# Norm rows and the stacks of attention B turned by transfers instead of by TensorE

## The chip, the cores and the metric
The kernel runs on one core of one Trainium2 chip. The metric is device time in microseconds (us), the time of one execution on that core. Five engines work side by side, each with its own instruction stream: TensorE (PE; its weight loads are listed as PEld), VectorE (DVE), ScalarE (ACT), GpSimd (POOL) and SyncE (SP), which here only issues transfers. They wait for each other through semaphores. All engines read and write the on-chip memory SBUF; PE writes its results to the eight banks of PSUM (`bank[0]` to `bank[7]`, 128 partitions x 512 float32 each).

## The reference, cut to what matters
The input x has 2 sequences of 512 tokens with 512 columns. Four layers are added to it in turn, each on the normalized rows of x:

```python
x = x + attention_a(_layernorm(x), ...)   # 32 heads of 128, 8 KV heads, weights as 4-bit codes with scales
x = x + ffn(_layernorm(x), ...)           # 8 experts of rank 64, the 2 best per token
x = x + attention_b(_layernorm(x), ...)   # 32 heads of 16, 8 KV heads
x = x + ffn(_layernorm(x), ...)           # the same experts once more
```

Attention B is `q, k, v = xn @ Wq, xn @ Wk, xn @ Wv`, a rotation of q and k (`q * cos + rotate_half(q) * sin`), causal softmax attention and `@ Wo`. The expert layer is `gate_probs = softmax(xn @ gate_w.T)`, the two largest of 8, and the weighted sum of `xn @ lora_A[e].T @ lora_B[e].T`.

## The kernel before, in words
**Tiles and precision.** The 1024 tokens are NT = 8 tiles of 128 rows (t = 0 to 7; ST = 4 per sequence). A matrix product takes the tokens as columns, so each normalized tile has to be turned from [128 tokens, 512] to four blocks [128 columns, 128 tokens]. Products run as three float16 products: each value is split into a high half (a float16 copy) and a low half (the value less the copy), and `three` issues high x high, high x low, low x high. `xt` holds the turned rows, halves `xt_hi` and `xt_lo`.

**Norm rows, for layer c = 0 to 3.** `ln_stats` (DVE) takes mean and variance, `ln_rsqrt` (POOL) the factor, `ln_norm` (DVE, L1549) writes the normalized tile to `xn` in SBUF. Then `ln_t` (PE, L1036) turns it by four transposes into a PSUM bank, `ln_hi` (ACT, L740) copies the bank to `xt_hi` and `ln_lo` (DVE, L1554) makes `xt_lo`.

**Order of work.** Each engine's order is written out by hand. First comes attention A, in groups j = 0 to 7, one per KV head; its probabilities are already turned by transfers on SP's queue (`turn_head`, L476: 20 blocks of 128 x 128 float16 each, from `p_row` to `p_turned`; the profile names these tiles `bw_hi` and `bw_lo`, with which they share memory). Its last products (`a_out`) are added to x by `o_add` (DVE) for t = 3 to 7.

Then `experts(0)`: for each t PE does `ln_t` of the next tile, the gate product (12 matmuls of 8 columns) and the product with `lora_a` (12 matmuls of 512 columns); ACT copies it to `hidden`. DVE chooses the experts for half of the tiles at a time (`gate_choice`, `gate_weights`), and POOL's `weighted` multiplies `hidden` by the weights into `hs` (L650). In a second loop PE turns `hs` back (`turn`, L1231) and multiplies by `lora_b` (`second`); DVE adds the result to x (`y_add`) and takes the next layer's statistics. On POOL, `largest` (L622) reduces the largest weight of a lot over the partitions, for the factors by which DVE's `w_factors` scales the weights; `w_scale` and `w_high` (ACT) and `w_low` (POOL, L630) then make the halves of the weights.

Then the projections of attention B. For each t PE computes `b_q` (12 matmuls of 512 columns) and `b_kv` (12 of 256). DVE's `rope_products` (L1922, L1923) makes the rotation's products in `rq1`, `rq2`, `rk1`, `rk2` (two buffers each, t % 2). POOL adds them (L678, L680). ACT's `stack_high` copies the high half twice to `q_stack` (L978) and four times to `k_stack` (L982), and POOL writes the low half twice to `q_stack` (L684) and four times to `k_stack` (L689). `stack_t` (PE, L1308) turns the 24 blocks in six units of four, through PSUM banks, and `stack_out` on ACT (L994) and DVE (L1931) copies them to `qt_b` and `kt_b`. Between the steps stand `ln_t`, `ln_hi` and `ln_lo` of tile t + 2 and the first score steps (`b_scores` on PE, `b_max` on DVE).

Then attention B itself runs in 16 sets q (sequence q // 8): `b_scores` and `b_max` find the row maxima, `b_split` (POOL) and `b_turn_max` turn them, `b_keys` and `b_exps` (ACT) make the probabilities in `pt`, and `b_pv` multiplies by v. The first `b_keys` with a maximum is the PE instruction of L1358 for set 0. The first sets need only the tiles 0 to 3. Last come the product with `b_o` and `experts(1)`, on rows of layer c = 3.

Of the kernel before, what the change touches and what calls it, by code (L numbers as in the profile page):

```python
# [24 lines left out]
P = 128  # L25
# [69 lines left out]
LN_BANK = [(0, 1, 0, 1, 6, 7, 6, 6), (2, 3) * 4, (3, 4) * 4, (3, 4) * 4]  # L95

HALF = NT // 2
GATE_BANK = [5, 7]
# [87 lines left out]


UNITS = 6
ACT_UNITS = (0, 1, 4, 5)


def t_bank(t, unit):

    return ((2, 7) if t < NT - 2 else (5, 7))[unit % 2]


def act_units(t, unit):

    before = len(ACT_UNITS) * min(t, NT - 2) + UNITS * max(t - (NT - 2), 0)
    return before + (unit + 1 if t >= NT - 2 else ACT_UNITS.index(unit) + 1)  # L200


def dve_units(t, unit):

    return 2 * t + unit - 1


def build(nc, t_in, out):
    ctx = ExitStack()
    with ctx:  # L210
# [85 lines left out]
        scn = sa("scn", [P, sum(QUANT_COLS.values())], F32)  # L296
# [8 lines left out]
        arena = sa("arena", [P, 10 * 1024], F32)  # L305
        q_hi = arena[:, 0:2048].bitcast(F16).rearrange("p (s n) -> p s n", s=8)
# [50 lines left out]
        rk1 = staged("rk1", [P, 2, P], F32)  # L357
        rk2 = staged("rk2", [P, 2, P], F32)
# [5 lines left out]
        ctx_t = sb("ctx_t", [P, S], F32)  # L364
# [42 lines left out]
        d_turned = [sem(f"d_turned{i}") for i in range(2)]  # L407
# [10 lines left out]
        bkept, zeros_done, bt_ps, bt_act, bt_dve = (sem(n) for n in ("bkept", "zeros_done", "bt_ps", "bt_act", "bt_dve"))  # L418
# [15 lines left out]
        def load_scales(eng, n, j):  # L434
# [13 lines left out]
        def _(sp):  # L448
# [41 lines left out]
        def _(pool):  # L490
# [142 lines left out]
            for t in range(ST):  # L633
                ln_rsqrt(1, t)
            w_low("lora_a", 0, 1)
            w_low("gate", 0, 1)

# [19 lines left out]
            for t in range(ST, NT):  # L657
                ln_rsqrt(1, t)
            w_low("lora_b", 0, 1)

            largest(1)
            pool.wait_ge(wlo_done, 3)
# [5 lines left out]
            pool.memset(bv[:, :, KV_HEADS * B_VD:], 0.0).then_inc(zeros_done, 1)  # L668
            weighted(0)
            w_low("b_o", 0, 1)  # L670
            for t in range(NT):
                ln_rsqrt(2, t)


            for t in range(NT):
# [39 lines left out]
            def b_keep(q, kt, loads):  # L715
# [3 lines left out]
                home = GROUP * (q % 2)  # L719
# [17 lines left out]
        def _(act):  # L737
            def ln_hi(c, t):
                act.wait_ge(xt_ps, NT * c + t + 1)
                act.activation(xt_hi[:, :, t * P:(t + 1) * P],  # L740
                               bank[LN_BANK[c][t]][:].rearrange("p (k n) -> p k n", k=KT),
                               ACT.Copy, scale=X_UP).then_inc(xthi_done, 1)

# [20 lines left out]
            for t in range(ST):  # L764
                ln_hi(0, t)
# [25 lines left out]
            def b_exps(q, which):  # L791


                home = GROUP * (q % 2)
# [54 lines left out]
            def group(j, first, last):  # L849
# [15 lines left out]
                if first:  # L865
                    ln_hi(0, ST + 3)
# [1253 lines left out]
```

## Time and profile before

| | us |
|---|---|
| median of 3 runs | 1022.82 (1020.14 to 1024.01) |
| the profiled execution, its own time | 1022.0 |
| its span, first to last instruction | 1020.3 |
| PE busy | 953.5 (93%) |
| DVE, POOL, ACT busy | 795.7, 629.8, 612.7 |

The times of all rows below are in us from the start of the span. Stretches, as the traced instructions mark them: attention A up to 693.6, experts(0) up to 751.7, projections of attention B up to 808.1 (the first `b_keys` with its maximum), attention B and its output up to 966.9, experts(1) up to the end. Busy time of an engine is not what sets the end: the chain of work that ended last, and the waits in it, do.

### The profile page before, as it was taken

Reading aid. Unit: us, or ns where it says so; the run is one execution under the profiler, and the core shown is the slowest. Engines: PE = TensorE matmul, PEld = TensorE weight load, DVE = VectorE, ACT = ScalarE, POOL = GpSimd, SP = SyncE. Lnnn points to the kernel's source line nnn. Section 1 sums busy time; section 2 is a strip of 40 time slices with the busy share of each in tenths; the row PEclk is TensorE's granted clock in tenths of the full one; section 3 lists DMA queues with packets and bytes.
Section 4 is the critical chain, followed back from the end, with each engine's and each line's share of the span. In section 5 each row is a group of like instructions: output and inputs, shape, how many; then the busy total and the mean of one; then the engine's idle time right before and its main releaser. Section 6 shows DMA issues by size and latency. Waiting matters only on the chain.

```text
span 1020.3 us, 20687 instructions
## 1 busy us (share of the span) xinstructions
PE 953.5 (93%) x7235; PEld 520.7 (51%) x7235; DVE 795.7 (78%) x1860; ACT 612.7 (60%) x1346; POOL 629.8 (62%) x643
## 2 busy tenths in 40 slices
PE   3698999999999999999999999868999799999998
PEld 1244555555555555555555555534456444444554
DVE  6877887887887887887888788758687789995744
ACT  2267666676666766667667665552637688886131
POOL 3767876967868768777777776213578444443111
PEclk9989999999999999999999999979999999999999
DMA  8164474364474473663653564520000000000002
GB/s 287 49 186 131 98 193 129 84 197 120 83 201 106 107 202 78 134 185 69 161 164 90 140 151 83 156 52 1 1 1 2 2 2 2 3 2 1 1 1 83
DMA packets 179892, 95.22 MB, mean 93 GB/s; under 512 B 168032, under 2 KB 168544, under 8 KB 175200
## 3 DMA queue, kind: packets, MB, share of 16 engines
q1 hardware_dynamic: 170016, 49.44, 22.3%
q10 hardware_dynamic: 9792, 44.59, 13.5%
q8 instruction: 62, 1.02, 0.4%
q14 instruction: 22, 0.18, 0.1%
HBM read 49.97 MB, written 2.10 MB: 51 GB/s over the span
## 4 chain that ended last, share of the span: by engine, by line
PE 76%; DVE 9%; POOL 5%; issue 5%; ACT 4%; DMA 1%; SPq 0%; ACTq 0%; DVEq 0%; POOLq 0%
PE bank L1026 15%; PE bank L1028 15%; PE bank L1027 15%; PE bank L1445 4%; PE bank L1113 3%; PE bank L1115 3%; PE bank L1114 3%; PE bank L1133 3%; PE bank L1135 3%; PE bank L1134 3%; PE bank L1353 2%; PE bank L1334 2%; PE bank L1358 2%; DVE bank L1656 1%; ACT bank L788 1%
## 5 line engine op out<-in xcount | busy, mean ns | idle before, releaser
L537 POOL TENSOR_TENSOR rt<-rt 128x512 f32<-128x512 f32 x80 | 101.1, 1268 | 137.8 <-DVE rt L1641 137.8
L1673 DVE SCALAR_TENSOR_TENSOR bw_hi<-bank,rden,bw_hi 128x128 f16<-128x128 f32 (+3 forms) x256 | 123.3, 544 | 61.3 <-ACT bw_hi L819 61.3
L788 ACT ACTIVATE bank<-bank,shift,c_score 128x128 f32<-128x128 f32 (+3 forms) x256 | 147.3, 605 | 2.1
L1656 DVE CUSTOM_DVE_ANT_0 bank<-bank,mask_w 128x512 f32<-128x512 f32 (+3 forms) x256 | 117.9, 518 | 21.7 <-PE bank L1115 21.4
L819 ACT ACTIVATE bw_hi<-bank,rden 128x128 f16<-128x128 f32 (+3 forms) x256 | 114.5, 536 | 25.3 <-DVE rden L1666 25.2
L783 ACT ACTIVATE shift<-smax,c_score 128x4 f32<-128x4 f32 x64 | 19.0, 297 | 163.3 <-DVE smax L1656 163.3
L1026 PE MATMUL bank<-xt,wq_hi 128*128 128x512 f16 x256 | 98.8, 386 | 2.2 <-DVE rt L1641 1.8
L1027 PE MATMUL bank<-xt,wq_hi 128*128 128x512 f16 x256 | 98.6, 385 | 0.0
L1028 PE MATMUL bank<-xt,wq_lo 128*128 128x512 f16 x256 | 98.5, 385 | 0.0
L1026 PE MATMUL bank<-wo_hi,arena 128*128 128x512 f16 x256 | 97.5, 381 | 0.6 <-DVE x L1685 0.6
L1027 PE MATMUL bank<-wo_lo,arena 128*128 128x512 f16 x256 | 97.5, 381 | 0.0
L1028 PE MATMUL bank<-wo_hi,arena 128*128 128x512 f16 x256 | 97.3, 380 | 0.0
L544 POOL TENSOR_TENSOR arena<-rt,arena 128x512 f16<-128x512 f32 x80 | 92.3, 1158 | 6.4 <-ACT arena L772 5.7
L800 ACT ACTIVATE pt<-bank,c_score_b 128x512 f32<-128x512 f32 x128 | 81.1, 686 | 19.9 <-PE bank L1358 19.5
L1113 PE MATMUL bank<-arena 128*128 128x512 f16 (+3 forms) x256 | 74.7, 304 | 16.5 <-DVE bw_hi L1673 8.7
L1133 PE MATMUL bank<-bw_lo,arena 128*128 128x512 f16 (+3 forms) x256 | 77.2, 302 | 7.5 <-DMA bw_lo<-bw_hi 7.1
L1114 PE MATMUL bank<-arena 128*128 128x512 f16 (+3 forms) x256 | 77.8, 304 | 0.0
L1134 PE MATMUL bank<-bw_lo,arena 128*128 128x512 f16 (+3 forms) x256 | 77.3, 302 | 0.0
L1115 PE MATMUL bank<-arena 128*128 128x512 f16 (+3 forms) x256 | 75.0, 304 | 0.0
L1135 PE MATMUL bank<-bw_lo,arena 128*128 128x512 f16 (+3 forms) x256 | 74.0, 302 | 0.0
L1639 DVE TENSOR_TENSOR rt<-bank,sin_a 64x512 f32<-64x512 f32 x80 | 55.4, 693 | 20.6 <-PE bank L1028 18.7
L1958 DVE TENSOR_REDUCE smax_b<-bank 128x2 f32<-128x1024 f32 (+1 forms) x64 | 58.6, 951 | 13.8 <-PE bank L1319 13.8
(235 smaller groups left out, 2597.1 us busy)
## 6 DMA issues: line engine op xcount, KB each, us to landing
qcode<-in_q_codes ACTq DMA_DIRECT2D x8, 1024.0 KB, 5.0
qscale<-in_q_scales ACTq DMA_DIRECT2D x8, 1024.0 KB, 7.8
ocode<-in_o_codes ACTq DMA_DIRECT2D x7, 1024.0 KB, 4.9
oscale<-in_o_scales ACTq DMA_DIRECT2D x7, 1024.0 KB, 8.7
kvcode<-in_k_codes ACTq DMA_DIRECT2D x8, 256.0 KB, 8.7
kvcode<-in_v_codes ACTq DMA_DIRECT2D x8, 256.0 KB, 9.0
kvscale<-in_k_scales ACTq DMA_DIRECT2D x8, 256.0 KB, 8.9
kvscale<-in_v_scales ACTq DMA_DIRECT2D x8, 256.0 KB, 9.2
```

Source lines behind the costliest of these rows:

```text
L788: act.activation(a_rows(i, s), a_rows(i, s), ACT.Exp, bias=shift[:, s % 2, c:c + 1], scale=c_score[:, 0:1], accum_out=bank[3][:, SUMS_AT + ...
L819: act.activation(p_row[:, s % 2, HI_AT[i]:HI_AT[i] + P_STEP * i + 1:P_STEP], turned_back(i, s), ACT.Copy, scale=rden[:, s % 2, c:c + 1]).t ...
L1026: pe.matmul(out_ap, a_hi, b_hi, start=(k == 0), stop=False)
L1027: pe.matmul(out_ap, a_hi, b_lo, start=False, stop=False)
L1028: return pe.matmul(out_ap, a_lo, b_hi, start=False, stop=(stop and k == n - 1))
L1113: pe.matmul(o_ap, q_hi[:, s, qs], k_hi[:, b, 0:w], start=True, stop=False)
L1114: pe.matmul(o_ap, q_hi[:, s, qs], k_lo[:, b, 0:w], start=False, stop=False)
L1115: mm = pe.matmul(o_ap, q_lo[:, s, qs], k_hi[:, b, 0:w], start=False, stop=True)
L1133: pe.matmul(o_ap, v_hi[:, b, vs], hi, start=(kt == 0), stop=False)
L1134: pe.matmul(o_ap, v_hi[:, b, vs], lo, start=False, stop=False)
L1656: dve.tensor_tensor_reduce(bank[bk][:, o:o + (i + 1) * P], bank[bk][:, o:o + (i + 1) * P], mask_w[:, S - (i + 1) * P:S], 1.0, LOWEST, ALU. ...
L1673: dve.scalar_tensor_tensor(out=p_row[:, s % 2, LO_AT[i]:LO_AT[i] + P_STEP * i + 1:P_STEP], in0=turned_back(i, s), scalar=rden[:, s % 2, c: ...
```

## The change
- `ln_norm` for c = 1 to 3 writes to a PSUM bank (`XN_BANK`), not to `xn`. `row_hi` (ACT) and `row_lo` (DVE) write both halves, still row by row, to the new SBUF tile `rows` (two buffers), and `turn_rows` turns a tile's 8 blocks by one transfer on SP's queue straight into `xt`. PE waits for the landing (`d_rows`). `ln_t`, `ln_hi` and `ln_lo` stay for c = 0 alone.
- In the projections `turn_stacks` turns `q_stack` (16 blocks) and `k_stack` (8 blocks) by two transfers into `qt_b` and `kt_b`. `stack_t`, both `stack_out` and `ident_h` are gone. A buffer of a stack is written again only when its transfer has landed (`d_q`, `d_k`).
- POOL makes the low half of the queries once (512 elements, not 1024), and ACT's new `stack_again` copies it to the second place.
- Orders change with it. `w_factors(0)` moves behind `probs_low(7)`; the reductions of the second lot of weights (`w_largest`) spread out; the second `largest` moves behind the memsets; `w_low` of `lora_a`, `lora_b` and `b_o` goes in quarters between the `ln_rsqrt`. The gate and weights of `experts` come in another order on DVE: `m_low` of the second tile goes ahead of the second `gate_weights`. The first three score steps' `b_max` run after all rotations, not between them.
- Memory: `rk1`, `rk2` and `ctx_t` move into `hs`, `scn` into `arena`, and the sets' places in `pt` are swapped so that set 0 doesn't touch the stacks.

```diff
+XN_BANK = {1: (3, 2), 2: (3, 4), 3: (4, 3)}
-GATE_BANK = [5, 7]
+GATE_BANK = [(7, 4), (5, 7)]
+        rows = sb("rows", [P, 2, 2, D], F16)
-        ident_h = sb("ident_h", [P, P], F16)
+        def rows_landed(c, t):
+            return 16 * (HALF * (c - 1) + t // 2 + 1)
...
+            def turn_rows(c, t):
+                sp.wait_ge(xt_done, NT * c + t + 1)
+                sp.dma_start_transpose(xt[:, :, :, t * P:(t + 1) * P].rearrange("p i k n -> p (i k) n"),
+                                       rows[:, t % 2].rearrange("p i n -> p (i n)")).then_inc(d_rows[t % 2], 16)
+            for t in range(NT):
+                turn_rows(1, t)
+            def turn_stacks(t):
+                ts = slice(t * P, (t + 1) * P)
+                sp.wait_ge(bq_lo, t + 1)
+                sp.dma_start_transpose(qt_b[:, :, ts], q_stack[:, t % 2]).then_inc(d_q[t % 2], 16)
+                sp.wait_ge(bk_lo, t + 1)
+                sp.dma_start_transpose(kt_b[:, :, ts], k_stack[:, t % 2]).then_inc(d_k[t % 2], 16)
+            for t in range(4):
+                turn_rows(2, t)
+            for t in range(NT):
+                if t + 4 < NT:
+                    turn_rows(2, t + 4)
+                turn_stacks(t)
+            for t in range(NT):
+                turn_rows(3, t)
...
-            largest(1)
-            pool.wait_ge(wlo_done, 3)
+            pool.wait_ge(wlo_done, 9)
             pool.memset(m_stack[:].rearrange("p i n -> p (i n)").bitcast(F32), 0.0).then_inc(zeros_done, 1)
...
+            largest(1)
             weighted(0)
...
-                rq = rq1[:, i2].rearrange("p (h d) -> p h d", d=B_HD).unsqueeze(2)
-                pool.tensor_tensor(st[:, :, 1], rq.broadcast_to([P, B_HEADS, 2, B_HD]), st[:, :, 0],
-                                   ALU.subtract).then_inc(bq_lo, 1)
+                pool.tensor_tensor(st[:, :, 1, 0], rq1[:, i2].rearrange("p (h d) -> p h d", d=B_HD), st[:, :, 0, 0],
+                                   ALU.subtract).then_inc(bq_once, 1)
...
+            def row_hi(c, t):
+                act.wait_ge(xn_ready, NT * c + t + 1)
+                if c > 1 or t >= 2:
+                    act.wait_ge(d_rows[t % 2], rows_landed(c, t) - 16)
+                act.activation(rows[:, t % 2, 0], bank[XN_BANK[c][t % 2]][:], ACT.Copy, scale=X_UP).then_inc(xthi_done, 1)
...
+            def stack_again(t):
+                act.wait_ge(bq_once, t + 1)
+                st = q_stack[:, t % 2].rearrange("p (h a e d) -> p h a e d", h=B_HEADS, a=2, e=2)
+                act.activation(st[:, :, 1, 1], st[:, :, 1, 0], ACT.Copy).then_inc(bq_lo, 1)
+            row_hi(2, 0)
+            row_hi(2, 1)
+            row_hi(2, 2)
             for t in range(NT):
...
+                if t + 3 < NT:
+                    row_hi(2, t + 3)
                 stack_high(t)
+                stack_again(t)
...
-            for t in range(ST, NT):
-                m_high(NT + t, 1.0)
+            row_hi(3, 0)
+            m_high(NT + ST, 1.0)
+            row_hi(3, 1)
+            m_high(NT + ST + 1, 1.0)
+            m_high(NT + ST + 2, 1.0)
+            row_hi(3, 2)
+            m_high(NT + ST + 3, 1.0)
+            row_hi(3, 3)
+            row_hi(3, 4)
             experts(1)
...
                 for t in range(NT):
-                    if t + 1 < NT and (ph == 0 or t):
-                        ln_t(c, t + 1)
-                    pe.wait_ge(xt_done, NT * c + t + 1)
+                    pe.wait_ge(d_rows[t % 2], rows_landed(c, t))
...
             for t in range(NT):
-                pe.wait_ge(xt_done, NT * 2 + t + 1)
+                pe.wait_ge(d_rows[t % 2], rows_landed(2, t))
...
-                wide(bank[t % 2][:], t, "b_q", D, range(0, 1))
-                if t >= 2:
-                    stack_t(t - 2, (2, 3))
...
+                wide(bank[t % 2][:], t, "b_q", D).then_inc(bq_ps, 1)
+                if t == NT - 1:
...
                     b_scores(0, 0, 3)
...
+            def row_lo(c, t):
                 dve.wait_ge(xthi_done, NT * c + t + 1)
+                dve.scalar_tensor_tensor(out=rows[:, t % 2, 1], in0=bank[XN_BANK[c][t % 2]][:], scalar=X_UP,
+                                         in1=rows[:, t % 2, 0], op0=ALU.mult, op1=ALU.subtract).then_inc(xt_done, 1)
...
                 row_factors(j, 7)
                 probs_low(j, 7)
                 ctx_low(j, "c", 5)
+                if last:
+                    w_factors(0)
...
+            row_lo(2, 2)
+            ln_norm(2, 3)
             for t in range(NT):
...
                 dve.wait_ge(bq_ps, t + 1)
                 if t >= 2:
                     dve.wait_ge(bk_lo, t - 1)
                 rope_products(bank[t % 2][:], rq1[:, t % 2], rq2[:, t % 2], t).then_inc(bq_mul, 1)
                 dve.wait_ge(bkv_ps, t + 1)
                 rope_products(bank[5 + t % 2][:, 0:P], rk1[:, t % 2], rk2[:, t % 2], t).then_inc(bk_mul, 1)
+                if t + 3 < NT:
+                    row_lo(2, t + 3)
+                if t + 4 < NT:
+                    ln_norm(2, t + 4)
+            b_max(0, 0, 3)
+            b_max(0, 0, 2)
+            b_max(0, 0, 1)
```

## Rows read from the trace of the kernel before

**Rows 1.** The page's part 4: shares of the chain that ended last.

```profile
PE 76%; DVE 9%; POOL 5%; issue 5%; ACT 4%; DMA 1%; SPq 0%; ACTq 0%; DVEq 0%; POOLq 0%
```

**Rows 2.** Windows view, two stretches: busy us (instructions) per engine, clock, DMA.

```profile
693.60:751.90 58.30, 52.85 (x362) 29.40 (x361) 46.15 (x113) 24.45 (x34) 29.68 (x30) 1.00 0.00 1
751.90:808.10 56.20, 52.23 (x482) 34.82 (x480) 41.17 (x88) 36.40 (x66) 42.09 (x38) 0.97 0.01 1
```

**Rows 3.** Timeline of PE, 669 to 723: start, us, instruction, [idle before <- releaser].

```profile
676.45 0.58 PE L1133 MATMUL bank<-bw_lo,arena 128*128 128x512 f16 x1 [7.08 <-DMA bw_lo<-bw_hi]
...
693.59 1.04 PE L1036 MATMUL bank<-ident,xn 128*128 128x128 f32 x8
...
696.33 0.18 PE L1026 MATMUL bank<-gate_hi,xt 128*128 128x8 f16 x1 [1.71 <-DVE xt L1554]
...
696.65 0.38 PE L1026 MATMUL bank<-lora_a_hi,xt 128*128 128x512 f16 x1
...
722.94 0.66 PE L1231 MATMUL bank<-ident,hs 128*128 128x128 f32 x4 [0.74 <-POOL hs L650]
```

**Rows 4.** Timeline of POOL around both partition reductions, same columns.

```profile
660.46 0.38 POOL L622 PARTITION_ALL_REDUCE pow_w<-amax_w  x1 [6.20 <-issue]
668.38 1.12 POOL L501 TENSOR_TENSOR rstd<-mv,minus_half 128x1 f32<-128x1 f32 x2 [7.54 <-DVE mv L1542]
...
712.19 0.39 POOL L622 PARTITION_ALL_REDUCE pow_w<-amax_w  x1 [11.85 <-DVE amax_w L1695]
...
720.38 1.24 POOL L665 TENSOR_TENSOR sel<-sel_f,one 128x640 bf16<-128x640 f32 x1 [7.54 <-issue]
```

**Rows 5.** Timeline of DVE ahead of row_factors(7) of the last group.

```profile
667.75 0.16 DVE L1526 TENSOR_SCALAR pow_w<-pow_w 128x3 f32<-128x3 f32 x1
...
668.94 0.15 DVE L1663 TENSOR_SCALAR rsum<-bank 128x4 f32<-128x4 f32 x1
```

**Rows 6.** The chain that ended last, in order of time: start, us, what.

```profile
733.26 0.44 PE bank L1231 x4
...
736.29 0.44 PE bank L1231 x4
...
756.05 1.28 POOL rq L678
```

**Rows 7.** Groups by form, POOL, 755 to 808 (busy us, mean ns, idle).

```profile
L684 POOL TENSOR_TENSOR q_stack<-rq,q_stack 128x1024 f16<-128x1024 f32 x8 | 17.1, 2134 | 5.9 <-ACT q_stack L978 5.9
L678 POOL TENSOR_TENSOR rq<-rq 128x512 f32<-128x512 f32 x8 | 10.3, 1290 | 2.6 <-DVE rq L1923 2.6
L689 POOL TENSOR_TENSOR k_stack<-rk,k_stack 128x512 f16<-128x512 f32 x8 | 9.3, 1158 | 0.0
```

**Rows 8.** Groups by form, ACT, the same stretch.

```profile
L978 ACT ACTIVATE q_stack<-rq 128x1024 f16<-128x1024 f32 x8 | 8.5, 1057 | 3.6 <-POOL rq L678 3.4
L982 ACT ACTIVATE k_stack<-rk 128x512 f16<-128x512 f32 x8 | 4.9, 618 | 0.0
```

**Rows 9.** Groups by form, DVE, the same stretch.

```profile
L1554 DVE SCALAR_TENSOR_TENSOR xt<-bank,xt 128x512 f16<-128x512 f32 x6 | 4.1, 681 | 0.0
```

**Rows 10.** All 64 transposing transfers: ns on SP's queue, and issue to landing.

```profile
L476 SPq DMA_TRANSPOSE bw_lo<-bw_hi x64: 2324/2587/10902, 52.3 to 672.2; - x64
...
DMA to landing us min/median/max: 4.1/4.3/13.1
```

**Rows 11.** Windows view, inside the landing of one such transfer.

```profile
674.00:675.00 1.00, 0.00 (x0) 0.00 (x0) 0.93 (x4) 0.00 (x0) 0.39 (x1) 0.50 1.27 290
```

**Rows 12.** Windows view, early in attention B.

```profile
814.00:820.00 6.00, 4.10 (x78) 2.43 (x74) 5.07 (x8) 5.06 (x8) 3.59 (x9) 1.00 0.00 0
```

**Rows 13.** Timeline of POOL: the last tile's low keys.

```profile
802.08 1.16 POOL L689 TENSOR_TENSOR k_stack<-rk,k_stack 128x512 f16<-128x512 f32 x1
```

**Rows 14.** Timeline of PE: set 0's first b_keys with its maximum.

```profile
808.09 0.39 PE L1358 MATMUL bank<-m_turned,sel 64*128 64x512 bf16 x2 [0.67 <-DVE m_turned L1965]
```

**Rows 15.** Timeline of DVE: the last m_low of the output product.

```profile
963.32 0.68 DVE L1861 SCALAR_TENSOR_TENSOR mt_lo<-bank,mt_hi 128x512 f16<-128x512 f32 x1
```

More of the change, by code:

```diff
@@ L930, in w_high @@
                 act.activation(w_hi[n][:], raw[n], ACT.Copy).then_inc(whi_done, 1)
-            for n in LOTS[0]:
-                w_scale(n)
-                w_high(n)
+            w_scale("lora_a")
+            w_high("lora_a")
+            row_hi(1, 0)
+            row_hi(1, 1)
+            ctx_high(KV_HEADS - 1, "cc", 7)
+            row_hi(1, 2)
+            w_scale("gate")
+            w_high("gate")
+            w_scale("lora_b")
+            row_hi(1, 3)
+            w_high("lora_b")
+            row_hi(1, ST)
             beside = [(w, n) for n in LOTS[1] for w in (w_scale, w_high)]
@@ L1327, in b_scores @@
                 at = STEP_AT[q, c, i]
+                if j == 0 and (c, i) in ((0, 3), (0, 2)):
+                    for i2 in range(2):
+                        pe.wait_ge(d_q[i2], 16 * ST // 2 * (b + 1))
+                        pe.wait_ge(d_k[i2], 16 * ST // 2 * (b + 1))
                 if at:
@@ L1778, in group @@
                 a_max(j, 6)
-                if not last:
+                if last:
+                    w_largest("b_q")
+                else:
                     rope(j + 1, ("k", 0))
@@ L1788, in group @@
                 o_add(j, "o", 1, last)
-                if last:
-                    w_factors(0)
-                else:
+                if not last:
                     rope(j + 1, ("q", 1))
@@ L1868, in y_add @@
                                          op0=ALU.mult, op1=ALU.add).then_inc(y_added, 1)
-            def y_adds(m0, scale, factor, after, t0=0):
-                for t in range(t0, NT):
-                    if t + 1 < NT:
-                        m_low(m0 + t + 1, scale)
-                    y_add(m0 + t, t, factor)
-                    if after is not None:
-                        dve.wait_ge(y_added, m0 + t + 1)
-                        ln_stats(after, t)
-                        if t == NT - 3:
-                            ln_norm(after, 0)
-                            ln_norm(after, 1)
-                        if t == NT - 2:
-                            ln_lo(after, 0)
-                            ln_lo(after, 1)
@@ L1909, in _, with y_stats, experts @@
-            experts(0, 2)
+            def y_stats(m, t, factor, after):
+                y_add(m, t, factor)
+                dve.wait_ge(y_added, m + 1)
+                ln_stats(after, t)
+            def experts(ph):
+                m0 = ph * 2 * NT
+                gate_choice(ph, 0)
+                gate_weights(ph, 0)
+                if ph == 0:
+                    w_factors(1)
+                m_low(m0, PROJ_DN_B)
+                gate_choice(ph, 1)
+                m_low(m0 + 1, PROJ_DN_B)
+                gate_weights(ph, 1)
+                for t in range(NT):
+                    if 0 < t < NT - 1:
+                        m_low(m0 + t + 1, PROJ_DN_B)
+                    if ph:
+                        y_add(m0 + t, t, c_ffn)
+                        continue
+                    if t >= 6:
+                        row_lo(2, t - 6)
+                    y_stats(m0 + t, t, c_ffn, 2)
+                    if 4 <= t < 7:
+                        ln_norm(2, t - 4)
@@ L2035, in _ @@
             m_low(NT + ST, 1.0)
-            y_adds(NT, 1.0, c_out_b, 3, ST)
-            experts(1, None)
+            ln_norm(3, 1)
+            for t in range(ST, NT):
+                if t + 1 < NT:
+                    m_low(NT + t + 1, 1.0)
+                out_add(t)
+                if t == 4:
+                    row_lo(3, 1)
+                if t == 5:
+                    ln_norm(3, 2)
+                if t == 6:
+                    row_lo(3, 2)
+            ln_norm(3, 3)
+            ln_norm(3, 4)
+            for t in range(3, NT):
+                row_lo(3, t)
+                if t + 2 < NT:
+                    ln_norm(3, t + 2)
+            experts(1)
 def constants():
```

328 lines of the change are left out of this document (132 added, 196 removed).

## The prediction
> **What bounds the kernel now.** I read the chain that ended last first: PE has 76% of it [rows 1], but the average hides where PE is not the limit, so the windows by stage, the waits and the timelines follow. Attention A, up to 669, and attention B, from 808 to 945, are left as they are but for their edges. The change sits in two stretches, 693.6 to 751.9 and 751.9 to 808.1, where PE is busy 52.85 of 58.3 and 52.23 of 56.2 us and the DMA engines do nothing (share 0.00) [rows 2]. In the first, PE works off its own list with pauses [rows 3]. In the second PE looks full, but the chain goes through POOL, ACT and DVE too [rows 6]: POOL's own list per tile is as long as PE's.
>
> **Part by part**, on the clock of the span.
>
> *End of attention A.* `w_factors(0)` stands ahead of `row_factors(7)` from 667.75 to 668.94 [rows 5]. The last probabilities, their transfer and PE's wait of 7.08 us [rows 3] hang on that; it moves behind: 1.2 us gained. The new `ln_norm`, `row_hi`, `row_lo` of the first tiles hide in DVE's and ACT's idle time during that wait and beside 14 us of `a_out`.
>
> *Start of experts(0).* From 693.59 to 696.33 PE turns two tiles and waits 1.71 us for `ln_lo` [rows 3]. By then rows 0 to 4 are turned already: 2.7 gained.
>
> *First loop.* It runs from 696.33 to 726.0 (four transposes and 12 matmuls after 722.94 [rows 3]), 29.7 us. A `second` with its `turn` takes 3.03 us, 0.44 of it the four transposes, so 12 matmuls of 512 columns take 2.59 [rows 6]; the 12 gate matmuls take 0.32 (696.33 to 696.65 [rows 3]). After: 8 x 2.91 + 0.44 = 23.7. But a new limit comes in on POOL. A partition reduction has 6.20 us without work ahead of it and 7.54 behind it, the latter in both cases [rows 4]. POOL gets to `largest(1)` at some 699 (last `lora_b` quarter, memsets, `sel`), reduces at 705.2, is free at 713, and `hs` of tile 0 (1.0 us) is there at 714; PE wants it at 712.9. That is a stall of 1.1, so the loop takes 24.8: 4.9 gained.
>
> *Second loop.* 726.0 to 751.7 before, 25.7 us. After, 8 x 3.03 - 0.44 = 23.8, plus 0.6 because DVE also has `ln_norm` for three tiles and one `row_lo` (0.68 [rows 9]) in its last rounds, plus 0.75 for the landing of row 0 of layer 2: 25.15. `row_lo(2, 0)` ends about 2 us before PE is ready for it, and the transfer takes longer. 0.5 gained. So `b_q` of tile 0 starts 1.2 + 2.7 + 4.9 + 0.5 = 9.3 us earlier.
>
> *Price of a transfer.* The trace only has 20-block ones: at least 2.32 us on SP's queue, 4.1 to landing [rows 10]; I see no two back to back. Low bound: the queue time scales, 0.116 us a block, and 1.8 is fixed. Then 8 blocks land in 2.7 and 16 in 3.7. High bound: 2.32 and 4.3 for every size. Per tile of the projections (8 + 16 + 8 blocks) that is 3.7 or 7.0 us of queue. I take the low one with 0.1 to 0.2 more per instruction, some 4.1, because each block is a run of descriptors of its own. The 1.05 MB per tile cost 3.6 us at the 290 GB/s inside one landing [rows 11]. The strided destination is new; a third more would be 4.8.
>
> *Projections.* Before, the eight tiles run from the first `rq` at 756.05 [rows 6] to the end of the last low keys at 803.24 [rows 13]: 47.2, 5.9 per tile. POOL's list per tile is 1.29 for `rq`, the wait for ACT's 1.06 (with `rk` inside), 2.13 for the low queries, 1.16 for the low keys [rows 7, 8]: 5.64. PE's is nearly as long, with 24 + 4 turned blocks between the products. After, PE has 2.59 + 1.3 = 3.9 (256 columns cost half). POOL's low queries have 512 elements, which cost 1.16 in the low keys [rows 7]: 1.29 + 1.16 + 1.16 + 1.16 (a hop of 0.1 in the second) is 4.77, with the last hop 4.8. ACT: 1.06 and 0.62 for the high halves, `row_hi` and the second copy at 0.5 to 0.7 each (the 0.62 of `k_stack` is the nearest, 0.6 taken), v, and a wait for POOL's low queries in between [rows 8]: 4.0. DVE has 41.17 us in the whole stretch now [rows 2] and loses `stack_out`; `ln_norm` to PSUM may cost 0.55 to 0.75 (0.68 taken, as `row_lo` [rows 9]): 3.5. SP's queue: 4.1. So POOL sets 4.8 per tile. Does a stack's buffer come free in time? `stack_high(t)` needs the landing for t - 2. From its own start it is 2.9 us to the second copy, then up to 2 us for SP (row transfer of t + 4 first), 3.7 to land: 8.6, against 9.6 for two tiles. One microsecond of slack; it is the thinnest place. 8 x 4.8 = 38.4: 8.8 gained.
> At the start, 0.75 is lost: DVE still has the last `y_add`, `row_lo(2, 2)` and `ln_norm(2, 3)` ahead of the first rotation. At the end, before, 4.85 from 803.24 to 808.09 [rows 14]. After, three `b_max` more stand behind the last rotation, alternating with PE, and end at the low keys' end + 1.2; split, turn, copy: 4.5. PE is mostly idle for some 12 us here, so I expect it at 1.2 GHz in the first `b_keys` and add 1.0: 5.5, 0.65 lost. Set 0 starts 9.3 - 0.75 + 8.8 - 0.65 = 16.7 earlier. Sets 1 to 15 are unchanged.
>
> *Output and experts(1).* Eight `ln_t` of 0.44 go: 3.5. But ACT's `m_high` of the last tile now stands behind `row_hi(3, 2)`, which waits for DVE's `ln_norm(3, 2)`, so the last `m_low`, at 963.32 before [rows 15], comes about 1.7 later than PE wants it. 1.8 gained.
>
> *Sum.* 16.7 + 1.8 = 18.5. The profiled execution took 1022.0 by its own time (span 1020.3), 0.8 under the median: 1003.5, and the median some 1004.
>
> **Rivals.**
> *A. The transfers set the pace.* If a block costs its share of a whole landing, 4.1 / 20 = 0.205 us, the 32 blocks take 6.6 per tile; if the queue price doesn't scale, three times 2.32 is 7.0 [rows 10]. Against 4.8 that is 14.4 to 17.6 lost: 1018 to 1021.5, no change. For it: 20 blocks are the only size seen. Against it: 2.32 is about the time in which 655 KB move at 290 GB/s [rows 11], so it looks paid by the block. A part of this (5 to 6 per tile) gives 1006 to 1013.
> The Trainium skill stands on this rival's side: VectorE: DVE Perf Modes, in its rules for kernel authors, wants 128 x 128 transposes on TensorE where PSUM will do, and its section on the three transpose paths gives 1309 ns for one block by transfer against 390. Block by block that would be 42 us per tile, some 300 us lost by that rule; the trace disagrees, with 20 blocks in 4.1 us, and leaves of it only what A says.
> *B. Transposing transfers of one queue don't overlap* (slower). Then a tile costs 2.7 + 3.7 + 2.7 = 9.1: 8 x 4.3 = 34 lost, 1038. It decides from 7.1 us per tile on. For it: the trace has no two in flight. Against it: a transfer leaves the queue after 2.32 to 2.59 and lands at 4.1 to 4.3 [rows 10], so the queue doesn't hold on to it.
> *C. PE falls to 1.2 GHz in the projections*, as it has pauses of 0.9 per tile: 7.8 per tile, 24 lost, 1028. Against it: 4.10 busy of 6.00 us at a full clock [rows 12], and that is less than 3.9 of 4.8.
> *D. The buffers of the stacks come back late*, by 1 us per tile: 8 lost, 1012, still faster.
>
> **How the numbers follow.** Forecast with D's milder forms (996 to 1012): 0.66. A in part or D in full (1012 to 1017.5): 0.06. A in full, 0.12. B 0.09, C 0.04. Still faster than 996: 0.03. The bound of 0.5% is 5.1 us, about what a measurement of this kernel can tell from no change. Faster, under 1017.7: 0.75; within it 0.12; slower 0.13. The likeliest case by itself has the range 998 to 1010. The 8 in 10: 996 to 1020; B, C and a part of A are left out above.
>
> **What would show it.** Right: gate 0 directly behind `a_out`; the reduction's 7.5 us then deciding when tile 0's `hs` comes; POOL's `rq` every 4.8 us; 8-block transfers under 1.3 us on SP's queue and 2.7 to landing; three transfers overlapping; set 0's `b_keys` near 791. Wrong: `q_stack` on ACT waiting for a landing; PE waiting for `d_rows` beyond tile 0 of a layer; a queue instruction of 2.3 us for 8 blocks; a granted clock under 1.0 in the projections before the last tile.

## The result and the profile after

The changed kernel takes 1007.81 us (median of 4 runs, 1006.78 to 1009.35), 0.9856 of the time before, 95% interval 0.9832 to 0.9881; the kernel before, timed beside it, has a median of 1023.20 in 4 runs. The profiled execution took 1006.78 us (span 1004.9) against 1022.0 (1020.3): 15.4 us less by the spans, where 18.5 were forecast. The chain that ended last, by engine, to be held against [rows 1]:

```profile
PE 74%; DVE 11%; POOL 5%; ACT 4%; DMA 3%; issue 3%; SPq 0%; ACTq 0%; DVEq 0%; POOLq 0%
```

DMA has 3% of it now, against 1%. The windows view of the stretches from the projections on (the last three columns are the granted clock, the DMA engines' share and GB/s), which answers to [rows 2]:

```profile
752.00:773.00 21.00, 17.64 (x110) 10.37 (x108) 11.89 (x35) 10.64 (x19) 15.67 (x16) 1.00 1.10 186
773.00:787.00 14.00, 6.96 (x69) 3.91 (x67) 7.48 (x14) 7.05 (x11) 10.07 (x10) 0.77 1.04 191
787.00:791.00 4.00, 2.48 (x24) 1.20 (x24) 3.67 (x6) 0.00 (x0) 1.16 (x5) 0.50 1.04 196
791.00:796.00 5.00, 3.94 (x48) 2.08 (x50) 3.97 (x7) 1.26 (x2) 0.00 (x0) 0.50 0.03 5
796.00:801.00 5.00, 3.74 (x38) 1.86 (x34) 2.39 (x4) 3.12 (x6) 1.00 (x5) 0.50 0.00 0
801.00:806.00 5.00, 3.90 (x68) 1.97 (x64) 4.99 (x8) 3.77 (x7) 2.60 (x5) 1.00 0.00 0
```

Two things stand out that the sum held only in part: the share of the 16 DMA engines is above 1 from 752 to 791, and PE runs at 1.2 GHz (0.50) up to 801, ten us into attention B. PE's timeline gives the marks of the stages: the last product with the values of attention A, gate 0 of experts(0), the first queries' product, the wait for the norm row of tile 6, the scores that wait 3.42 us behind the last products, the first subtraction of the maxima [rows 14], the last tile of the output product, and tile 3's product in experts(1).

```profile
675.07 0.59 PE L1169 MATMUL bank<-bw_lo,arena 128*128 128x512 f16 x1 [5.85 <-DMA bw_lo<-bw_hi]
691.11 0.17 PE L1063 MATMUL bank<-gate_hi,xt 128*128 128x8 f16 x1
741.15 0.38 PE L1063 MATMUL bank<-bw_hi,xt 128*128 128x512 f16 x1 [0.98 <-DMA xt<-rows]
772.15 0.39 PE L1063 MATMUL bank<-bw_hi,xt 128*128 128x512 f16 x1 [2.82 <-DMA xt<-rows]
780.44 0.50 PE L1349 MATMUL bank<-kt_b,qt_b 64*128 64x384 f16 x2 [3.42 <-DVE smax_b L1960]
791.11 0.61 PE L1373 MATMUL bank<-m_turned,sel 64*128 64x512 bf16 x2 [0.57 <-DVE m_turned L1967]
950.33 0.39 PE L1063 MATMUL bank<-bw_hi,mt_hi 128*128 128x512 f16 x1 [1.54 <-DVE mt_lo L1882]
963.10 0.39 PE L1063 MATMUL bank<-lora_a_hi,xt 128*128 128x512 f16 x1 [0.72 <-ACT hidden L980]
```

In the projections, first SP's queue from the stacks of tile 0 to the queries of tile 2 (start, us on the queue), then POOL's `rq` of the tiles 0, 1, 2, 3 and the last low keys (compare [rows 6, 13]), then what ACT's high queries waited for (us in total, times, longest):

```profile
752.27 2.22 SPq L478 DMA_TRANSPOSE qt_b<-q_stack  x1
754.53 1.61 SPq L480 DMA_TRANSPOSE kt_b<-k_stack  x1
756.18 1.32 SPq L468 DMA_TRANSPOSE xt<-rows  x1
757.54 2.75 SPq L478 DMA_TRANSPOSE qt_b<-q_stack  x1
760.34 1.32 SPq L480 DMA_TRANSPOSE kt_b<-k_stack  x1
761.70 1.33 SPq L468 DMA_TRANSPOSE xt<-rows  x1
763.08 1.64 SPq L478 DMA_TRANSPOSE qt_b<-q_stack  x1
```

```profile
745.50 1.26 POOL L691 TENSOR_TENSOR rq<-rq 128x512 f32<-128x512 f32 x1 [2.02 <-DVE rq L1932]
750.17 1.26 POOL L691 TENSOR_TENSOR rq<-rq 128x512 f32<-128x512 f32 x1
754.84 1.27 POOL L691 TENSOR_TENSOR rq<-rq 128x512 f32<-128x512 f32 x1
760.15 1.26 POOL L691 TENSOR_TENSOR rq<-rq 128x512 f32<-128x512 f32 x1
...
785.32 1.16 POOL L701 TENSOR_TENSOR k_stack<-hs,k_stack 128x512 f16<-128x512 f32 x1
```

```profile
ACT q_stack L1016 <- DMA qt_b<-q_stack: 7.9, 4, 2.8
```

The queue has no gap: each row transfer, 1.3 us long, starts where the keys' one ends. A tile is 5.2 to 5.5 us of queue. POOL's `rq` comes every 4.67 us where nothing is late (tiles 0 to 2) and 5.2 to 5.9 us apart for the next four tiles, because the high queries of a tile go into the buffer that the transfer two tiles back still reads.

Every later comparison goes by stages, since one execution reaches gate 0 up to 7 us later than another of the same code up to there (688.43 in all_more, 695.08 in all_four_again). The columns, in us, each the difference of two times in a timeline: **A** gate 0 of experts(0) to the first queries' product; **B** first `rq` to the end of the last low keys; **C** from there to the first subtraction of the maxima; **D** from there to the first values product of set 1; **E** from there to gate 0 of experts(1); **F** from there to the last turned tile.

The medians are from several chips; each kernel's ratio is to the kernel before on its own chip.

| kernel | gate 0 at | A | B | C | D | E | F | median, all runs |
|---|---|---|---|---|---|---|---|---|
| before | 696.33 | 55.4 | 47.2 | 4.9 | 20.1 | 138.7 | 44.4 | 1022.8 |
| after | 691.11 | 50.0 | 41.0 | 4.6 | 22.2 | 139.6 | 43.0 | 1007.8 |
| after, again | 693.32 | 49.9 | 40.8 | 4.3 | 22.4 | 139.6 | 42.9 | 1008.8 |
| rows_only | 691.95 | 50.0 | 45.6 | 5.2 | 21.9 | 139.5 | 41.8 | 1010.8 |
| pool_both | 691.47 | 49.9 | 45.1 | 3.0 | 22.2 | 139.6 | 43.0 | 1009.5 |
| rows_one | 691.67 | 50.0 | 40.2 | 4.1 | 22.2 | 139.6 | 42.8 | 1007.6 |
| rows_pe | 692.38 | 50.1 | 37.4 | 4.5 | 22.2 | 139.6 | 41.8 | 1002.9 |
| stacks_first | 694.44 | 49.9 | 39.7 | 7.0 | 22.6 | 139.6 | 42.8 | 1008.3 |
| warm_b | 696.29 | 50.4 | 40.9 | 4.1 | 20.1 | 139.6 | 41.8 | 1005.1 |
| warm_a | 693.69 | 50.2 | 40.2 | 4.6 | 22.6 | 139.6 | 41.8 | 1006.8 |
| late_rows | 691.83 | 50.0 | 40.8 | 4.3 | 22.4 | 138.4 | 41.8 | 1004.7 |
| all_four | 692.90 | 50.5 | 37.4 | 4.5 | 21.6 | 138.4 | 41.8 | 1000.7 |
| all_four, again | 695.08 | 50.7 | 37.4 | 4.5 | 21.8 | 138.4 | 41.8 | 999.9 |
| all_more | 688.43 | 52.7 | 37.4 | 4.4 | 20.1 | 138.4 | 41.8 | 999.0 |

### The profile page after: what moved, and what is told of

Read it like the earlier page. It is cut to its first block, busy times and chain, and to the rows that moved or that the text cites. A ratio compares the mean times of both kernels' runs of the same rounds, so it can differ in the third digit from the quotient of the medians.

```text
span 1004.9 us, 20128 instructions
## 1 busy us (share of the span) xinstructions
PE 932.7 (93%) x6947; PEld 500.0 (50%) x6947; DVE 786.9 (78%) x1847; ACT 598.1 (60%) x1318; POOL 620.5 (62%) x652
## 4 chain that ended last, share of the span: by engine, by line
PE 74%; DVE 11%; POOL 5%; ACT 4%; DMA 3%; issue 3%; SPq 0%; ACTq 0%; DVEq 0%; POOLq 0%
PE bank L1063 14%; PE bank L1064 14%; PE bank L1065 14%; PE bank L1441 4%; PE bank L1149 3%; PE bank L1151 3%; PE bank L1150 3%; PE bank L1169 3%; PE bank L1170 3%; PE bank L1171 3%; PE bank L1368 2%; PE bank L1349 2%; PE bank L1373 2%; DMA qt_b<-q_stack 1%; DVE bn L1532 1%
```

## The experiments

**Half of the change alone (rows_only).** Norm rows by transfer; the stacks are turned by PE again and the low queries written twice by POOL, in the order of the kernel before.

```diff
-                turn_stacks(t)
...
+                if t >= 2:
+                    stack_t(t - 2, (2, 3))
...
-                stack_again(t)
+                    stack_out(t - 1, (0, 1))
```

> Norm rows by transfer, stacks turned by PE and copied out by ACT and DVE, both low halves by POOL, all as in the kernel before. My account: all that the first part gains (10.55 us until the first product of queries) stays, the projections take POOL's old list again, 5.6 to 5.9 us per tile instead of 5.1, and the 2.1 us that attention B now loses at its start with PE at 1.2 GHz come back, as PE has the turned blocks to do. Span 1020.3 - 10.7 - 0.5 = 1009, so 4 us over the changed kernel, of which the old list costs 6.2 and the clock gives back 2.1. Rival (in the projections before it was PE that set the pace, with 0.44 us of turned rows per tile that are gone here): 5.4 per tile and a span of 1005 to 1006, so that the second part is worth nothing.

Measured: span 1009.4, ratio to before 0.9870 (0.9846 to 0.9894). POOL's `rq` every 5.64 us, the own list as forecast, B 45.6. So the turned rows carry most of the change. By the stages the second part is worth 3.6 to 4.0 us (B to F against the two profiles of the changed kernel), 4.6 of it in the eight tiles; of the 8.8 us of gain that the sum has there, 6.2 came, and 1.6 of those belong to the turned rows. The ratios put it at 1.4 us with intervals of 2.5 to each side, so they can't tell it from nothing. One point of the expectation fell: the 2.1 us did not come back. D stayed at 21.9, as the clock dropped here too, with the turned blocks on PE, and twice:

```profile
792.00:798.00 6.00, 5.25 (x51) 3.42 (x52) 4.31 (x7) 3.14 (x7) 1.17 (x5) 0.50 0.02 4
799.00:801.00 2.00, 0.91 (x24) 0.54 (x22) 2.00 (x3) 0.09 (x1) 0.00 (x0) 1.00 0.00 0
802.00:808.00 6.00, 4.75 (x48) 2.42 (x42) 3.94 (x6) 4.04 (x7) 2.38 (x7) 0.50 0.01 3
```

**Low halves written by POOL (pool_both).**

```diff
-                pool.tensor_tensor(st[:, :, 1, 0], rq1[:, i2].rearrange("p (h d) -> p h d", d=B_HD), st[:, :, 0, 0],
-                                   ALU.subtract).then_inc(bq_once, 1)
+                rq = rq1[:, i2].rearrange("p (h d) -> p h d", d=B_HD).unsqueeze(2)
+                pool.tensor_tensor(st[:, :, 1], rq.broadcast_to([P, B_HEADS, 2, B_HD]), st[:, :, 0],
+                                   ALU.subtract).then_inc(bq_lo, 1)
...
-                stack_again(t)
```

> POOL writes both low halves of the queries (1024 elements, 2.13 us) and ACT's copy goes; all else as in the changed kernel. POOL's list per tile is 5.64, longer than what the transfers need (5.3 to 5.5 with rows, 3.7 without), so rq comes every 5.64 us, the eight tiles take 45.6 instead of 41.0, and the waits for the buffer of the query stack vanish: span 1009.5. Rival (the transfers' waits add to POOL's list instead of hiding in it): 47 to 50 for the eight tiles, span 1011 to 1014.

Measured: span 1007.6, ratio 0.9868 (0.9849 to 0.9886). B is 45.1, the eight lists of 5.64 and nothing on top: at that pace the transfers are hidden. But C fell from 4.6 to 3.0, which I had not foreseen. The maxima of set 0 follow DVE's last rotation and not the end of POOL's list: the first `b_max` starts 2.5 us later than in the changed kernel (781.55 against 779.08), the last low keys end 4.4 later. Of the 4.1 us that the single low half saves in the loop, 1.7 are given back behind it.

**Bytes or transfers? (rows_one, rows_pe, stacks_first).** `rows_one` leaves out seven of the eight blocks of each row transfer of tiles 4 to 7 of layer 2:

```diff
+                n = 1 if c == 2 and t >= 4 else 8
-                sp.dma_start_transpose(xt[:, :, :, t * P:(t + 1) * P].rearrange("p i k n -> p (i k) n"),
-                                       rows[:, t % 2].rearrange("p i n -> p (i n)")).then_inc(d_rows[t % 2], 16)
+                sp.dma_start_transpose(xt[:, :, :, t * P:(t + 1) * P].rearrange("p i k n -> p (i k) n")[:, 0:n],
+                                       rows[:, t % 2].rearrange("p i n -> p (i n)")[:, 0:n * P]
+                                       ).then_inc(d_rows[t % 2], 16)
```

> Left out: seven of the eight blocks of each row transfer of tiles 4 to 7 of layer 2 (values there are old ones). The number of transfers and their order are the same, the bytes of a tile in the first half of the projections fall from 1.05 to 0.82 MB. Theory 1 (bytes: the 16 DMA engines are full, 110% of them from 752 to 773, and 1.05 MB at 190 GB/s are 5.5 us a tile): a tile needs 4.3 us of them, less than POOL's list of 4.67, the waits of the query stack for its buffer (7.9 us in all) go, rq comes every 4.7 us and the last low keys end at 782.8 instead of 786.5: 3.5 us gained, span 1001.4. Theory 2 (a price per transfer on SP's queue, or the order in it): the same three instructions per tile, 5.3 us of queue again, no gain beyond 0.5: span 1004.4 to 1004.9.

Measured: span 1003.9, ratio 0.9847 (0.9824 to 0.9870). B is 40.2: 0.8 gained of 3.5 (0.6 against the second profile of the changed kernel). Theory 1 fell in its pure form. SP's queue in this run, and the DMA share (last but one column) beside it:

```profile
757.76 2.06 SPq L480 DMA_TRANSPOSE qt_b<-q_stack  x1
759.86 1.69 SPq L482 DMA_TRANSPOSE kt_b<-k_stack  x1
761.60 1.23 SPq L469 DMA_TRANSPOSE xt<-rows  x1
```

```profile
757.00:762.00 5.00, 5.00 (x33) 2.94 (x32) 2.98 (x9) 2.97 (x5) 3.76 (x5) 1.00 0.85 159
762.00:767.00 5.00, 5.00 (x31) 2.86 (x30) 3.00 (x10) 2.97 (x5) 3.79 (x5) 1.00 0.85 160
```

One block costs the queue 1.13 to 1.51 us, as much as eight (1.23 to 1.42), and with the engines' share down to 0.85 a tile still takes 5.1 us of queue. So what the row transfer costs the queue is the price of having it there, not of its blocks. For the stacks this does not follow: 16 blocks take 2.07 us in the median.

`rows_pe` takes the row transfer of those tiles away altogether and lets PE turn them:

```diff
-                if t + 4 < NT:
-                    turn_rows(2, t + 4)
...
+                if 1 <= t and t + 3 < NT:
+                    xn_turn(t + 3)
```

> The rows of tiles 4 to 7 of layer 2 are turned by PE again (four 128x128 of float32 each, 0.44 us, behind the keys' products of tiles 1 to 4), split by ACT and DVE into the same tiles. Bytes: as in the run with one block, but with one transfer less per tile. PE has 3.9 + 0.44 = 4.35 us per tile, under POOL's 4.67. Theory 1 (bytes): 3.5 gained, span 1001.4. Rival (ACT or PE is pushed over POOL's pace by the turned rows, since ACT has to wait for PE's transposes ahead of the high halves): 1 to 2 gained only, or none.

Measured: span 1001.3, median 1002.93, ratio 0.9805 (0.9781 to 0.9828). `rq` comes every 4.67 us from the first to the last tile, B is 37.4: all of the 3.6 us, with PE busy 5.00 of 5.00 us in the windows up to 772. DVE's rotations waited for PE four times, 3.5 us in all, but none of it reached POOL, whose `rq` waited for nothing after the first. Two `rq` in a row, tiles 2 and 3, beside POOL's own list of 4.67:

```profile
756.15 1.27 POOL L691 TENSOR_TENSOR rq<-rq 128x512 f32<-128x512 f32 x1
760.82 1.26 POOL L691 TENSOR_TENSOR rq<-rq 128x512 f32<-128x512 f32 x1
```

`stacks_first` changes only the order in the queue:

```diff
-                if t + 4 < NT:
-                    turn_rows(2, t + 4)
                 turn_stacks(t)
+                if t + 4 < NT:
+                    turn_rows(2, t + 4)
```

> SP's queue has the two stack transfers of a tile ahead of the row transfer of the tile four on, not behind it. Theory 2 (order: a stack waits for 1.3 us of queue behind rows, and its buffer is back that much later): 1.3 us per tile less from the high halves to the landing, the waits for the buffer (2 us per tile) nearly go, 3 gained, span 1002. Theory 1 (bytes): the engines are as full as before, the stacks land earlier and the rows later by the same, PE then waits for rows more than the 3.4 us in all that it waits now (0.55 and 2.82 us, tiles 5 and 6): gain under 1, or a loss of up to 2.

Measured: median 1008.32, ratio 0.9849 (0.9824 to 0.9874), as the changed kernel. `rq` keeps 4.67 us for six tiles, and then PE waits for rows, 1.36, 1.11 and 2.17 us; B is 1.3 shorter, C 2.3 longer. The wait moved from the stack's buffer to the rows.

One thing stayed unparted. At the 212 GB/s that the stacks alone reach in rows_pe the 1.05 MB of a tile take 5.0 us; with one block in place of eight the queue takes 5.1. So in the changed kernel both the engines and the queue are over POOL's 4.67, near each other, and no run has all the bytes without the third transfer.

**The clock (warm_b, warm_a).** Extra products in PE's waits, whose results nobody reads. There are 30 of them, not the 28 of the expectation:

```diff
+            def keep(n, bk=7):
+                for _ in range(n):
+                    pe.matmul(bank[bk][:], xt_hi[:, 0, 0:P], xt_hi[:, 0, 0:S], start=True, stop=True)
+            keep(14)
             b_scores(0, 0, 2)
+            keep(5)
             b_scores(0, 0, 1)
...
```

> 28 extra products of 512 columns (0.22 us each at 2.4 GHz, into a bank that nobody reads) fill PE's waits between the last keys' products of the projections and the first keys of attention B; nothing else is changed. Theory (the clock: PE runs at 1.2 GHz from 780 to 801 because it was idle from 777, and that makes the start of attention B 2.1 us longer): the granted clock stays at 1.00, the stretch from the first subtraction of the maxima to the second set's first values product falls from 22.2 to 20.1 us, and the last low keys to the maxima from 4.6 to 4.0. Span 1004.9 - 2.7 = 1002.2. Rival (the new order of the three b_max behind the last rotation, or the later layout of ACT's loads, costs the 2.1, not the clock): clock 1.00, 22.2 as before, span 1004.9 or a little more, as the extra products stand in the way.

Measured: median 1005.06, ratio 0.9805 (0.9780 to 0.9830). The windows of the same stretch, the clock now 1.00:

```profile
792.00:795.00 3.00, 2.14 (x27) 1.04 (x26) 2.99 (x5) 0.00 (x0) 1.18 (x5) 1.00 0.88 164
795.00:798.00 3.00, 1.90 (x30) 0.89 (x28) 2.34 (x4) 1.27 (x2) 0.00 (x0) 1.00 0.56 106
798.00:801.00 3.00, 1.40 (x26) 0.79 (x26) 3.00 (x6) 0.40 (x1) 0.00 (x0) 1.00 0.00 0
```

D is 20.1, to the tenth what it was before the change, and C 0.5 shorter (0.2 against the second profile). The rival is out: the order of the maxima is the same here. (This profiled execution reached gate 0 at 696.3, so its span, 1006.5, hides that; the stages and the median show it.)

`warm_a` puts 24 such products ahead of the last product with the values of attention A, where PE waits for a transfer.

> 24 such extra products between the last but one and the last product with the values of attention A, where PE waits 5.85 us for a transfer. The last product with the values takes 3.1 us at 1.2 GHz there; at 2.4 GHz 1.6. If the clock is what it costs: gate of tile 0 1.5 us earlier, span 1003.4. If the clock needs a longer past than these 5 us: nothing.

Measured: median 1006.78, ratio 0.9835 (0.9817 to 0.9854). The clock holds, and from that product to gate 0 it is 15.8 us against 16.0 in the first profile of the changed kernel and 17.1 in the second. So the gain is 0.2 to 1.3, depending on when the clock comes back by itself; part of the rest goes into a new wait of 1.08 us for DVE's addition.

**The last third (late_rows).**

```diff
-            row_hi(3, 2)
             m_high(NT + ST + 3, 1.0)
+            row_hi(3, 2)
...
+        def row_buf(c, t):
+            return more_rows[:, t % 2] if c == 3 and t % 4 >= 2 else rows[:, t % 2]
```

> Two edits in the last third: ACT's high half of the last tile of the output stands ahead of the high halves of the norm row 2, and the norm rows of layer 3 have four buffers instead of two. Theory: the first takes away PE's wait of 1.54 us ahead of the last product of the output, and the second ACT's waits for a landing (4.36 and 2.64 us), behind which the evictions of the first products stand (PE 0.15 + 0.72 us, and the last turn 1.2 us later than in the run with four tiles turned by PE, whose rows landed 1.4 us sooner): from the second set's first values product to gate 0 of layer 3 139.6 becomes 138.1, from there to the last turn 43.0 becomes 41.8. Span 1004.9 - 2.7 = 1002.2. Rival (DVE, in order, comes to row 2 later and passes the wait on): the first gives under 0.5.

Measured: span 1002.8, median 1004.74, ratio 0.9819 (0.9800 to 0.9837). PE's wait ahead of the last output product:

```profile
949.41 0.39 PE L1073 MATMUL bank<-bw_hi,mt_hi 128*128 128x512 f16 x1 [0.29 <-DVE mt_lo L1895]
```

0.29 instead of 1.54, E 1.2 shorter. It is the first edit that does this: in the changed kernel `row_hi(3, 2)` waited 4.66 us for DVE's norm row, not for a landing. F came to 41.8, as forecast, but four kernels with two buffers have 41.8 too. The nine profiles with two buffers fall into two groups. In five (the changed kernel twice, pool_both, rows_one, stacks_first) ACT waits 4.2 to 4.4 us for the first landing, PE then 0.72 for `hidden`, and F is 42.8 to 43.0; in four (rows_only, rows_pe, warm_b, warm_a) the longest such wait is 2.8 to 3.0, PE waits for nothing, and F is 41.8. So the buffers can take away a loss of 1.2 us that about half of these profiles have; why one falls into either group is open.

**All together (all_four, all_more).**

> The four edits that gained something, together: tiles 4 to 7 of layer 2 turned by PE, PE kept busy in both waits, the last high half of the output first, four row buffers in layer 3. If the causes are separate, the stage terms add up: 3.6 (projections) + 0.5 and 2.1 (clock) + 1.3 (output) + 0 to 1.2 (rows of layer 3) + 0.2 to 1.2 (end of attention A) = 7.7 to 9.9 off the changed kernel: span 995 to 997.2, median 998 to 1000. If the faster projections only lengthen PE's wait behind them (DVE's maxima were hidden by POOL, as in the run with both low halves by POOL), the first two terms give 4 instead of 6.2: 997 to 999.

> The changed kernel once more, on the same chip as the combination: 1007 to 1009 us. Stages (gate 0 of layer 1, first queries' product, rq 0, last low keys, maxima, second set's values, gate 0 of layer 3, last turn): 50.0, 4.4, 41.0, 4.6, 22.2, 139.6 as before; the last, 43.0 in its first profile and 41.8 to 43.0 in the others, depends on how soon the third row of layer 3 lands, and may come out at 42 to 43.

> The combination with eight more extra products, two in each of PE's four waits behind the first subtraction of the maxima (0.52, 0.62, 0.69 and 0.78 us long in the combination, two products are 0.43). In the combination the clock still fell, at 794, and the stretch from the maxima to the second set's values took 21.6 us against 20.1 in the run in which it held. Theory (clock alone): it holds, 20.1, the stretch before it as in the combination (4.5): 1.4 us off the combination, span 998.9. If something else set the 21.6, no gain.

> The combination of four once more, beside it on the same chip: 1000 to 1001 us; if the clock falls at 794 again, 21.6 for that stretch, if not, 20.1.

Measured: the combination of rows_pe, warm_a, warm_b and late_rows takes 1000.65 us on the chip on which the changed kernel takes 1008.83 (ratios to before 0.9770, 0.9750 to 0.9790, and 0.9856, 0.9835 to 0.9877), and 999.85 on another (0.9780, 0.9756 to 0.9803). Its span was 1000.3, three above the forecast: gate 0 came 1.8 later than in the profile it was reckoned from, and D stayed at 21.6, as the clock fell again at 794. In the second profile of the same kernel it fell again, near 795, and D was 21.8. With eight products more (all_more) D is 20.1, and the time 999.03 (0.9772, 0.9750 to 0.9794). That stage fits to a tenth; in the medians the 0.8 us are within what the runs can tell.

In all_more gate 0 came earliest of all, at 688.43, and A grew by 2.7. This is the limit that the prediction had put into the first loop: POOL's second reduction and then `hs` of tile 0, for which PE now waits 1.87 us. Behind that wait the clock fell too (0.50 from 711 to 714), which makes up the rest. Five other runs (rows_pe, warm_b, warm_a, the combination twice) have 0.20 to 1.27 us of the same wait. PE's and POOL's rows of that run:

```profile
710.98 1.09 PE L1287 MATMUL bank<-ident,hs 128*128 128x128 f32 x4 [1.87 <-POOL hs L672]
```

```profile
701.66 0.38 POOL L637 PARTITION_ALL_REDUCE pow_w<-amax_w  x1 [6.23 <-ACT hidden L996]
709.80 2.04 POOL L672 TENSOR_TENSOR hs<-hidden,wfull 128x512 f32<-128x512 f32 x2 [7.76 <-issue]
```

## Why the prediction was nearly right, and where it was not

Direction and mechanism held; the profiled execution came out 3.3 us above the 1003.5 of the sum. That it came so close is in part luck: four terms came out worse than forecast by 6.7 us in all, and the others better by 3.6, of which 1.1 is no gain of the change. Step by step, forecast against measured:

| step | forecast gain | measured |
|---|---|---|
| end of attention A | 1.2 | 1.4, and 1.1 more by the clock |
| start of experts(0) | 2.7 | 2.7 |
| first loop | 4.9 | 5.6 |
| second loop | 0.5 | -0.2 |
| start of the projections | -0.75 | 0.0 |
| eight tiles | 8.8 | 6.2 |
| end of the projections | -0.65 | +0.2 |
| sets 0 and 1 of attention B | 0 | -2.1 |
| sets, output and experts(1) | 1.8 | 0.5 |
| sum | 18.5 | 15.4 |

*End of attention A, first loop.* The wait for the last probabilities fell from 7.08 to 5.85 us, and to 5.89 in the second profile: 1.2, as forecast. The 1.4 of the table is a difference of two absolute times; in the second profile that product starts at 676.27, only 0.2 earlier than before, so it is not firmer than such times are. The 1.1 more is the clock, which in the windows of 2 us is back at 678 (0.98) instead of 682 (1.00); in the second profile of the same kernel it did not come back sooner (17.1 us to gate 0, as before), so it is no gain of the change. POOL began its second reduction 2.2 us earlier than I put it (its last writes ended at 696.8, not 699), so there was no stall, with 0.2 us to spare: `hs` of tile 0 is there at 711.6, and PE takes it at 711.75. The two prices were right: 6.10 us ahead of the reduction and 7.30 behind it [rows 4], and all_more shows the stall once PE comes earlier.

*Second loop.* PE waits 0.35 and 0.16 for `mt_lo` of the tiles 1 and 2, as ACT has the scaling of a weight ahead of the high half, 0.36 in the last round and 0.98 for the first row's landing. The last two were in the sum, the others not.

*The eight tiles.* This is the term that was mis-sized. POOL's 4.67 was right (4.8 forecast), and so was its place as the limit, for three tiles. What failed is the 4.1 us of queue per tile, and with it the microsecond of slack of the stack's buffer that the text called the thinnest place. Measured: 8 blocks of rows 1.23 to 1.42 us (0.93 plus 0.1 to 0.2 taken), 16 blocks 1.64 at best and 2.07 in the median (1.86 plus 0.1 to 0.2 taken), the keys behind them 1.68 in the median, 5.2 to 5.5 in all. The low bound scaled one row, 20 blocks in 2.32 us [rows 10], through zero; one block at 1.13 to 1.51 shows that the line has a foot. Landings were 0.3 to 0.7 longer than taken (3.0 and 4.4). So tiles 1 to 3 waited 2.9 to 3.3 us from the second copy of the queries to the start of their transfer, where the text allowed 2. The engines' rate failed as well. The 290 GB/s of [rows 11] hold for two microseconds of a 20-block landing, but the new transfers run mostly at some 210 (single microseconds reach 256 to 289), even where the queue leaves them gaps (first the kernel before, then the stacks in rows_pe, then one row transfer alone in the changed kernel):

```profile
673.50:675.50 2.00, 0.00 (x0) 0.00 (x0) 1.55 (x4) 0.00 (x0) 0.55 (x1) 0.50 1.27 289
752.50:756.00 3.50, 3.50 (x26) 2.41 (x25) 2.39 (x7) 2.47 (x4) 2.93 (x4) 1.00 1.13 212
739.50:740.00 0.50, 0.50 (x4) 0.10 (x1) 0.47 (x3) 0.00 (x0) 0.19 (x1) 1.00 1.11 214
```

At 212 GB/s the 1.05 MB of a tile take 5.0 us, near the 4.8 that the text had as "a third more" for the strided destination and left out of the sum; back to back, at 186 to 196, they take 5.4 to 5.6. Whether the destination is the cause no run shows. The text also saw no two transfers back to back in the trace before; there are such pairs, as at 132.16 and 143.16, and there the first is 10.90 us on the queue. So rival A held in part and D was its form: the buffer's wait, 7.9 us in four tiles, and PE's wait for the rows of tiles 5 and 6 (0.55 and 2.82) cost B the 3.6 us that rows_pe gets back. B is out: a queue instruction starts every 1.3 to 3.3 us, a landing takes 3.0 to 5.4.

*Start and end of the projections.* The 0.75 was not lost: `rq` follows the first product by 4.35 us in both. At the end PE was at 1.2 GHz as forecast, and the chain through the maxima was still 0.9 shorter than the 5.5 put down.

*Sets 0 and 1.* "Sets 1 to 15 are unchanged" failed. The clock was seen to fall, but its price was put at 1.0 for the first `b_keys` alone, as if the work itself would bring it back at once. It stayed at 0.50 until 801, and that cost 2.1 us in D. `warm_b` and `all_more` show the cause: at 1.00 the stage takes 20.1. The trace before has only a short fall in the same place, 0.54 and 0.61 from 801 to 805 (it is what makes the 0.97 of [rows 2]), and rival C was about the projections themselves, where the clock was indeed 1.00 up to the last product.

*Output and experts(1).* The wait of 1.54 us for the last tile (1.7 forecast) is there, and late_rows shows that the order on ACT was its cause. Missing in the sum was the same thing in the loop: `h_out` (ACT's copy to `hidden`) stands behind `row_hi` on ACT, which waited 4.36 and 2.64 us for a landing. Six of the eight `ln_t` lie in F, so 44.4 less 2.6 is 41.8, which the second group above has; the changed kernel was 1.2 over it in both profiles. The line "PE waiting for `d_rows` beyond tile 0" in the list of signs was the right one to look at, but I had taken it for the projections.

The case that came is the forecast with D's milder form.

## What to carry to other kernels

Price a new transfer by its fixed part first: on this queue it is 1.2 us even for one block, so one transfer less per round gained 3.6 us where seven eighths of its bytes gained 0.8. Where a step is taken off PE, ask what PE does in the gaps and what its clock will be behind them; here the gap at the end of the projections was paid in attention B. And where an in-order engine gets a wait for a landing, list what stands behind it: both edits of late_rows are about that.

## What the runs showed of the hardware beyond that

- The new transposing transfers, back to back on one queue, move 186 to 196 GB/s with the engines' share at 1.04 to 1.10, and 212 to 214 with gaps between them; those of 20 blocks into `p_turned` reach 289.
- A transfer of one 128 x 128 block and one of eight take the queue the same: 1.13 to 1.51 and 1.23 to 1.42 us. The Trainium skill (VectorE: DVE Perf Modes, its section on the three transpose paths) prices one block by transfer at 1309 ns, close to what a single one costs the queue here; but the trace has eight of them in 3.0 us to landing and sixteen in 4.4, so the figure can't be multiplied.
- PE fell to 1.2 GHz at the end of 3.4 us of waiting and stayed there for 20 us with PE about 65% busy, then rose; with extra products it held 2.4 GHz through the same stretch. In the first combination it held through the waits and fell 5 us behind the last extra product. In rows_only it fell, rose and fell again within 11 us.
- The second partition reduction: 5.8 to 6.2 us without work ahead of it and 6.8 to 7.9 behind it in the thirteen profiles of the changed kernel and its variants; 7.54 behind it before the change.
